# Perceiver with two cross attentions: value-product waves issued in pairs, once per eight key tiles

## The reference, cut to what matters

```python
energy = jnp.einsum('nqhd,nkhd->nhqk', q, k)               # 512 queries x 8192 keys
energy = jnp.where(mask == 0, jnp.float32(-1e+20), energy) # first layer only
attention = jax.nn.softmax(energy / jnp.sqrt(jnp.float32(EMBED)), axis=3)
out = jnp.einsum('nhql,nlhd->nqhd', attention, v).reshape(n, q_len, EMBED)
return out @ Wo.T + bo
```

## Time and profile before

| | |
|---|---|
| median of 3 runs | 4158.3 us (4152.01 to 4160.54) |
| profiled execution: span | 4154.8 us |
| PE busy | 3803.5 us, 92% |
| DVE / ACT / POOL busy | 68% / 56% / 45% |
| L0 heads, first to last L727 | 444.9 to 1384.4 us |
| L1 heads, first to last L727 | 2446.9 to 3285.1 us |

### The profile page before, as it was taken

One profiled execution on the slowest core, in us unless ns is written; L12 is line 12 of the kernel. 1 busy time (PEld: TensorE's weight loads), 2 busy tenths in 40 slices (PEclk: granted clock), 3 DMA queues, 4 the chain that ended last, 5 costly groups with the idle time before them and its releaser, 6 DMA issues. The chain is left out here.

```text
span 4154.8 us, 51637 instructions
## 1 busy us (share of the span) xinstructions
PE 3803.5 (92%) x17986; PEld 2240.3 (54%) x17986; DVE 2806.4 (68%) x3506; ACT 2342.3 (56%) x3654; POOL 1867.7 (45%) x1116
## 2 busy tenths in 40 slices
PE   7998999999999975789999779999999988769998
PEld 6886444444444342257888534444444435447886
DVE  4332877777777268946888667777777453568888
ACT  2222777777777734423777426666666630437775
POOL 0000487887878719910000148888888810000001
PEclk9998999999999987989999969999999997789999
DMA  8996576666666521023888657777777531218887
GB/s 309 332 341 235 123 159 153 154 155 152 156 154 151 126 81 56 0 96 132 320 321 323 239 143 172 175 173 170 171 174 173 126 79 52 61 52 325 322 319 268
DMA packets 295660, 750.49 MB, mean 181 GB/s; under 512 B 55630, under 2 KB 89166, under 8 KB 260842
## 3 DMA queue, kind: packets, MB, share of 16 engines
q1 hardware_dynamic: 246522, 570.48, 41.3%
q0 software_dynamic: 48880, 176.71, 21.4%
HBM read 476.62 MB, written 98.96 MB: 139 GB/s over the span
## 5 line engine op out<-in xcount | busy, mean ns | idle before, releaser
L861 ACT ACTIVATE prob<-psum 128x512 f32<-128x512 f32 x1628 | 917.7, 598 | 397.4 <-PE psum L746 365.0
L1045 POOL TENSOR_TENSOR den_pool<-den_pool,prob 128x1024 f32<-128x1024 f32 x405 | 1021.5, 2522 | 83.0 <-DVE den_pool L960 31.9
L746 PE MATMUL psum<-q_stack,k_ring 98*128 98x512 f32 x2048 | 958.9, 499 | 19.9 <-ACT prob L861 16.6
L931 DVE CUSTOM_DVE_ANT_0 psum<-psum,mask_q 128x1024 f32<-128x1024 f32 x512 | 627.4, 1235 | 240.2 <-PE psum L708 224.3
L927 DVE TENSOR_REDUCE row_max<-psum 128x1 f32<-128x1024 f32 x512 | 609.6, 1220 | 242.1 <-PE psum L708 237.7
L708 PE MATMUL psum<-k_ring,q_stack 96*128 96x512 f32 x2048 | 670.1, 410 | 35.2 <-DMA k_ring<-k_lo 18.4
L746 PEld LDWEIGHTS psum<-q_stack,k_ring 98*128 98x128 f32 x2048 | 394.8, 193 | 523.8 <-ACT psum L867 199.2
L1868 DVE TENSOR_TENSOR weight_lo<-weight_raw,weight_hi 128x2048 fp32r<-128x2048 f32 x180 | 411.4, 2290 | 113.9 <-ACT weight_hi L1864 113.7
L757 PE MATMUL psum<-prob,x 128*32 128x512 f32 x3256 | 472.9, 605 | 2.9 <-ACT prob L861 0.8
L708 PEld LDWEIGHTS psum<-k_ring,q_stack 96*128 96x128 f32 x2048 | 390.9, 195 | 122.8 <-issue 34.6
L2043 POOL DMA_DIRECT2D y_slots<-xnT x28 | 15.4, 550 | 860.6 <-ACT xnT L2147 860.6
(11 more groups left out here) (459 smaller groups left out, 6616.0 us busy)
## 6 DMA issues: line engine op xcount, KB each, us to landing
den_dma<-prob POOLq DMA_DIRECT2D x211, 512.0 KB, 5.0
k_ring<-k_hi SPq DMA_DIRECT2D x1024, 64.0 KB, 2.3
weight_raw<-in_L_ffn_Wu SPq DMA_DIRECT2D x60, 1024.0 KB, 7.1
weight_raw<-in_L_ffn_Wd SPq DMA_DIRECT2D x60, 1024.0 KB, 5.3
weight_raw<-in_L_ffn_w SPq DMA_DIRECT2D x60, 1024.0 KB, 6.6
den_dma<-xnT POOLq DMA_DIRECT2D x72, 512.0 KB, 5.0
k_ring<-k_lo SPq DMA_DIRECT2D x512, 64.0 KB, 2.6
w_o<-in_L_ffn_w SPq DMA_DIRECT2D x30, 1024.0 KB, 7.2
```

The source lines that it names most:

```text
L746: e.matmul(out, k_ring[:, n % kring, kt * P:(kt + 1) * P], q_stack[h % n_q][:], start=not masked, stop=True, skip_group_check=masked and b ...
L861: e.activation(prob[b // 2 % n_p][:, b % 2, :], bank_of("block", b), ACT.Exp, scale=scale).then_inc(s_exp, 1)
L931: e.tensor_tensor_reduce(out=max_banks(q), in0=max_banks(q), in1=masks[0][:, i, 2 * c2 * KC:2 * (c2 + 1) * KC], scale=1.0, scalar=-3.0e38, ...
L1045: e.tensor_tensor(den[:], den[:], tile, ALU.add).then_inc(s_dpool, 1)
```

## The change

`wave_step(w)` is now the same for an even w and the odd one after it. Waves 0 and 1 are both issued at step 4, waves 2 and 3 at step 8, and so on to 14 and 15 at step 32. The even wave comes two steps later than before, the odd one where it was. Each wave keeps its own waits, and `sum_wave` still follows its wave. `Banks` and ACT's `take_values` and `take_sums` read the same function.

```diff
 def wave_step(w):
 
-    return 2 * w + 2
+    return 2 * (w | 1) + 2
```

## The result

The changed kernel takes 4205.8 us (median of four runs, 4203.1 to 4210.5) against 4155.2 us before on the same chip: a ratio of 1.0122, 95% interval 1.0108 to 1.0137. The forecast was 4210 us, slower. The profiled execution has a span of 4208.3 us, 53.5 us more than before.

What follows compares the result with a forecast made beforehand. PE, 99% and 98% busy in the heads, was taken to set the pace. Exposed waits outweigh saved switches: 2.2 us a head in L0, 1.3 in L1, by 15 heads, 33 + 19 = +52 us, giving 4210 us, range 4180 to 4231.

Steps and rivals of the forecast that it cites:

- What a pair saves: PE's switches into and out of column groups: each merged pair saves 0.31 us in L0, 0.33 in L1, without waits.
- The fill in L0: Steps 2, 6, 10, 14, 22, 26: PE waits for ACT's mask fill, net +0.23 us each, 1.4 us a head.
- DVE's additions: Four additions at steps 3 to 6 of L0: no new cost; the one late maxima per head stays.
- Steps 29 to 32: Head's end without wave 14 at step 30: +0.80 us in L0 (fill, maxima row), +0.88 in L1 (row maxima wait).
- The reductions in L1: Steps 5 to 8, 9 to 12, 13 to 16: fourth maxima wait for DVE, +0.13 us each, +0.4 a head.
- Steps 1 to 4 and 21 to 28 in L1: Three four-step stretches taken at zero, each between -0.33 us (no stall) and +0.13.
- The sum: Both attentions: 33 us in L0 plus 19 in L1, +52 us on the profiled span, 4210 us expected.
- The last head of L0: Left at zero, as it has neither maxima nor row maxima; L0's cost counted for 15 heads.
- The last head of L1: Given no cost; L1's 1.3 us a head was counted for 15 heads only.
- Rival A: Only PE's pitches count, no waits, in both layers: 72 us faster, 4086 us; chance 0.07.
- B: Stalls and saved switches cancel: no change, within 8 us of 4158; chance 0.04.
- C: L0's ring: POOL falls behind, ACT and PE wait, 40 us in addition, about 4250 us; chance 0.03.

Runs made afterwards that it cites:

- e4: The changed kernel with L1's DVE reductions over 512 of 1024 columns: 4170.4 us, ratio 1.0039 to the kernel before.
- e5: The kernel before (waves one at a time) with L1's DVE reductions over 512 of 1024 columns: 4152.6 us, ratio 0.9995 to the kernel before.
- e3: The changed kernel with ACT's mask fill in L0 ahead of the exponential where the bank is free: 4183.1 us, ratio 1.0059 to the kernel before.
- e7: The kernel before with pairs in L0 and no ACT fill there (PE adds every mask), L1 one at a time: 4170.3 us, ratio 1.0035.
- e2: The changed kernel with wave 14 back at step 30 in both layers, seven pairs a head: 4179.2 us, ratio 1.0051 to the kernel before.
- e6: The kernel before (waves one at a time) with no ACT fill in L0, PE adding every mask: 4186.3 us, ratio 1.0074.

## Why the prediction was right, point by point

- **What a pair saves** (0.31 in L0, 0.33 in L1): nearly right in L1, where e4 against e5 gives 0.29 with short reductions. In L0 the parts hold where the filled block follows; e3 leaves -0.11 with 0.1 of lateness and 0.10 for the late block's pitch, so again 0.31.
- **The fill in L0** (+0.23 at six places): measured +0.23 in four columns, +0.28 at steps 1-4 and +0.10 at 5-8. The last is low because the kernel before had a wait for DVE there, its column is 0.13 longer than the neighbours', and the new stall absorbs it. I had said that it stays. It does come back where the fill isn't waited for (e3, e7), so DVE's additions are a cost of the pairs that the forecast had at nothing; the fill's stall covered it.
- **Steps 29 to 32** (+0.80 in L0, +0.88 in L1): +0.74 and +0.84, shown by e2.
- **The reductions in L1** (+0.13 at three places): +0.08. The waits came as worked out; the second wave of a pair is 0.02 us cheaper than the lone wave by which I priced it, and the rest is rounding of pitches. e4 shows the cause.
- **Steps 1 to 4 and 21 to 28 in L1** (zero): -0.08 and -0.14, within the bounds given.
- **The sum**: 33 + 19 was forecast for fifteen heads each. A head measured 2.0 us more in L0 (2.2 forecast) and 0.8 in L1 (1.3), and the stretches 29.6 and 12.1. What filled it up again was a step I had at zero, the last heads, and time outside the attentions. So the mechanism was right, but that the total came within 5 us of the forecast is in part luck.
- **The last head of L0** (zero): between the last L727 and the last wave L0 takes 64.9 us instead of 61.5, of which 0.74 are steps 29 to 32 of the head before. Without maxima PE reaches the filled block sooner and waits longer, eight times here for 6.8 us in all by the view of waits (1413 to 1478 us), where the kernel before has one such wait of 1.0 us; that the last head has no row maxima was no reason to leave it at zero. In the changed kernel:

```profile
1431.92 0.50 PE L746 MATMUL psum<-q_stack,k_ring 98*128 98x512 f32 x1 [0.78 <-ACT psum L867]
```

- **The last head of L1** (zero): 63.2 us instead of 59.3, of which 0.84 are the steps 29 to 32. Most of the rest is TensorE's clock, not a wait. The stretch from the last L727 to the last wave, before and changed (the clock is the third number from the end), then a pair in the changed kernel:

```profile
3285.10:3344.41 59.31, 51.81 (x277) 17.09 (x280) 2.13 (x3) 39.22 (x74) 41.17 (x24) 0.97 0.51 111
```

```profile
3331.76:3394.93 63.17, 56.76 (x277) 18.89 (x280) 2.13 (x3) 38.79 (x74) 41.56 (x25) 0.92 0.48 104
3343.93:3347.09 3.16, 3.16 (x18) 0.60 (x17) 0.00 (x0) 0.70 (x2) 3.16 (x4) 0.58 1.03 395
...
3343.93 3.23 PE L757 MATMUL psum<-prob,x 128*32 128x512 f32 x16
3347.09 0.50 PE L746 MATMUL psum<-q_stack,k_ring 98*128 98x512 f32 x1
```

Within these stretches the granted clock is 1.00 (2.4 GHz) but for short spells at half (1.2 GHz), three in the changed kernel and one before; the pair shown takes 3.16 us instead of 1.86. From 3340 to 3343 us, ahead of the fall, PE was busy for 2.3 of 3.0 us at a clock of 1.00. Other executions order themselves by the number of spells: none and 58.0 us in e6 (mean clock 1.00, waves one at a time in L1), two and 61.6 us in e3 (0.94, L1's code as in the changed kernel). A spell thus costs some 1.6 us, and about 3 of the 3.9 us are the clock's. Whether the pairs bring on more spells by the gaps that they leave, or whether it is chance, no run shows. In L0 the mean clock of the last head is 0.97 in both kernels.

- That makes 49 us in the attentions. The other 4.7 us of the spans' difference lie in stages that the change doesn't touch. The stretch between L0's and L1's rows took 1068.1 us in the changed kernel and 1063.2 in e4, whose L0 is the same code: that much two executions differ there.
- **Rival A** (72 us faster) failed because the waits came in. Without the fill, or with short reductions, the pairs do gain, but half or less of A's price: 13 us in L0's stretch (e7 against e6), 17 in L1's (e4 against e5). **B** and **C** had nothing: no wait of ACT for a wave or for POOL shows up in L0 between 500 and 1380 us.

Not tried: a second bank for the filled block, or a third pair for the maxima; the kernel already uses eight PSUM banks (0 to 7) and has none left for them.

## What to carry to other kernels

On an engine that is 98 or 99% busy, a block of work that others don't depend on is also the cover under which they catch up. Before moving it, look at what stands behind it at its old place and when its releaser ends: here the fill ended 0.38 us after PE's natural arrival, and at the head's edge the row maxima's low part was ready only just in time. That decided the sign. Doubling the distance between covers asks for buffers that last twice as long; L1's two pairs of maxima did not. When one wait is removed the next may show: behind the fill stood DVE's additions. And part of the saving, 7 us in L0, was there to take once one instruction of ACT stood one place earlier and one wave stayed where it was.

## What the runs showed of the hardware that I had not expected

A switch from column groups back to the whole array has no fixed price. The pitch of a lone wave is 1.00 us instead of 0.88 whichever block follows (605.30 to 606.30 in the kernel before, 655.18 to 656.18 in e6), but the block behind pays 0.11 us more if it begins with L746 (0.34 against 0.23; weight load 0.19 us) and nothing if it begins with the mask matmul (0.46 either way; weight load 0.10 us). In a pair the first wave has a pitch of 0.88 us, as ahead of the head output, and the second 0.97 to 0.98 rather than the 1.00 of a lone one.

The clock isn't 1.00 throughout. In a last head of L1, where PE is busy for 52 to 57 us of 59 to 63, there were one to three short spells at half clock in the kernels with pairs in L1 and none or one in the others, and one of them costs more than any single wait that the forecast counted.
